# Self attention of a post-norm decoder layer: query and key projections issued in halves of the contraction, all projections spread over sixteen blocks

## What is computed

```python
# x, ctx: (8, 512, 256) float32; 16 heads of 16 channels
x = layernorm(x + self_attention(x, w_qkv, w_proj, b_proj, rel_bias_table))
x = layernorm(x + cross_attention(Q=x, K=ctx, V=ctx))      # no projections
x = layernorm(x + expert_ffn(x, centroids, ...))           # 8 experts, one for each token

def self_attention(x):
    qkv = x @ w_qkv.T                                       # (8, 512, 768)
    q, k, v = split into 16 heads of 16
    scores = q @ k.T * 0.25 + bias(rel_bias_table, distance)
    return softmax(scores) @ v @ w_proj.T + b_proj
```

## Time and profile before

| what | value |
|---|---|
| median of 3 runs | 1048.36 us (1044.22 to 1048.89) |
| span of the profiled execution, first to last instruction | 1045.2 us |
| PE busy | 934.1 us (89% of the span) |
| ACT busy | 747.5 us (72%) |
| DVE busy | 703.3 us (67%) |
| mean granted clock of TensorE | 0.951 of 2.4 GHz |
| self attention, by the first exponential of its batches | 37.3 to 418.5 us |
| cross attention | 418.5 to 715.5 us |

### The profile page before, as it was taken

The page is one execution under the profiler, slowest core; times in us unless marked ns, Lnnn a source line. Parts: engine busy times, 40 slices in busy tenths (PEclk is TensorE's granted clock), DMA queues, the critical chain, the costliest instruction groups (busy, mean ns, idle before and its releaser), DMA issues. The chain is left out here.

```text
span 1045.2 us, 17700 instructions
## 1 busy us (share of the span) xinstructions
PE 934.1 (89%) x5301; PEld 514.6 (49%) x5301; DVE 703.3 (67%) x1836; ACT 747.5 (72%) x1414; POOL 297.5 (28%) x337
## 2 busy tenths in 40 slices
PE   5599999999999999999999998996189999999991
PEld 2133444444444433333333333332179988988991
DVE  5277777677787788356556565585457887887883
ACT  1378777787878778899898895893047766766761
POOL 4043132231404111011222123123323534444443
PEclk9699999999999999999999997997589999999996
DMA  7989596978687675987876793751263533443450
GB/s 208 207 229 251 109 256 143 316 142 252 143 247 187 185 201 88 181 199 161 160 155 114 157 174 68 144 120 41 76 216 115 202 137 121 169 180 127 163 208 30
DMA packets 74844, 172.04 MB, mean 165 GB/s; under 512 B 16657, under 2 KB 36039, under 8 KB 64712
## 3 DMA queue, kind: packets, MB, share of 16 engines
q1 hardware_dynamic: 67944, 156.36, 60.4%
q0 software_dynamic: 6496, 14.16, 3.9%
q10 hardware_dynamic: 320, 0.52, 0.1%
HBM read 122.23 MB, written 53.73 MB: 168 GB/s over the span
## 5 line engine op out<-in xcount | busy, mean ns | idle before, releaser
L742 ACT ACTIVATE probs<-sc 128x512 f32<-128x512 f32 x1024 | 528.9, 608 | 117.7 <-DVE sc L829 80.4
L497 PE MATMUL sc<-qst,kst 57*128 57x512 f32 (+1 forms) x1024 | 268.4, 473 | 18.2 <-DMA qst<-s_qk 12.8
L829 DVE TENSOR_TENSOR sc<-sc,strip 128x308 f32<-128x308 f32 (+1 forms) x512 | 192.8, 430 | 101.2 <-PE sc L497 100.5
L509 PE MATMUL ot<-probs,vals 128*32 128x512 f32 x1600 | 214.0, 607 | 0.1
L497 PEld LDWEIGHTS sc<-qst,kst 57*128 57x128 f32 (+1 forms) x1024 | 118.6, 187 | 191.8 <-ACT probs L742 147.7
L1691 ACT ACTIVATE f_h<-f_h_ps,par 128x384 f32<-128x384 f32 x104 | 60.9, 586 | 31.0 <-PE f_h_ps L1601 31.0
L1768 DVE TENSOR_TENSOR f_h_lo<-f_h,f_h_hi 128x384 fp32r<-128x384 f32 x104 | 73.4, 706 | 13.7 <-DVE f_h_hi L1766 5.7
L1849 POOL DMA_INDIRECT home<-s_x,get_ids x45 | 53.6, 1190 | 72.5 <-issue 42.4
L1766 DVE CAST f_h_hi<-f_h 128x384 fp32r<-128x384 f32 x104 | 37.1, 356 | 39.7 <-ACT f_h L1691 39.5
L509 PE MATMUL ms<-probs,vals 128*32 128x512 f32 x448 | 61.9, 627 | 0.0
L1862 POOL DMA_INDIRECT out<-f_normed,f_put_ids x39 | 43.1, 1106 | 64.6 <-ACT f_normed L1725 56.1
(11 more groups left out here) (189 smaller groups left out, 1604.7 us busy)
## 6 DMA issues: line engine op xcount, KB each, us to landing
s_qk<-w_hi SPq DMA_DIRECT2D x32, 512.0 KB, 7.3
strip<-in_w_all SPq DMA_DIRECT2D x16, 1024.0 KB, 7.7
f_raw<-in_w_all SPq DMA_DIRECT2D x14, 1024.0 KB, 6.3
s_x<-x SPq DMA_DIRECT2D x8, 1026.0 KB, 11.0
kst<-s_qk SPq DMA_DIRECT2D x32, 256.0 KB, 6.1
qst<-s_qk SPq DMA_DIRECT2D x32, 256.0 KB, 7.2
s_x_parts<-split SPq DMA_DIRECT2D x16, 512.0 KB, 8.8
kst<-s_ctx_parts SPq DMA_DIRECT2D x32, 256.0 KB, 6.6
```

Source lines behind the costliest of these rows:

```text
L497: nc.tensor.matmul(sc[j][:], kst[at:at + rows, i, P * c:P * c + P], qst[at:at + rows, i, :], start=True, stop=True).then_inc(scored, 1)
L509: last = nc.tensor.matmul(sums_bank(n, g)[32 * j:32 * j + 32, :], vals[:, c, 4 * g + j, :], probs[:, k % KEPT, j, :], start=(c == 0), stop ...
L742: nc.scalar.activation(probs[:, k % KEPT, j, :], sc[j][:], ACT.Exp, scale=scale).then_inc(exped, 1)
L829: nc.vector.tensor_tensor(sc[j][:, lo:hi], sc[j][:, lo:hi], band_backwards(rank_of(4 * g + j), at, hi - lo), ALU.add).then_inc(biased, 1)
```

## The change

Seven things move, and nothing of the arithmetic is left out:
- A q or k tile is made in two parts, one half of the contraction at a time, in two different blocks. Tiles i = 0 and 1 of the next batch take blocks 0 to 3, tiles 2 and 3 blocks 12 to 15.
- ACT and DVE split these tiles in blocks 2, 4 and 15, and the last one in block 0 of the next batch. The store of tiles 2 and 3 and the load of pair 1 move behind it, into the batch that uses them.
- The v projections take blocks 8 to 11 and the output projection blocks 4 to 7, one block earlier each, and the DVE work behind them moves with them.
- The second group of transposes, `turn_x1(b, 0)`, moves from block 15 to block 1 of the next batch, with its copies in block 2.
- The x of batches 2 to 7 is loaded into the memory of `x2` (`later_xT`), and is split by halves behind `copy_v` on GpSimd.
- The last v tile and the transposes go through `ms2`.
- The waits on `ms` banks follow.

```diff
@@ -156,6 +156,7 @@
         x_hi, x_lo = sb("x_hi", [P, DC, N], F32R), sb("x_lo", [P, DC, N], F32R)
         w_qkv_lo = sb("w_qkv_lo", [P, DC, 3 * C], F32R)
         x2 = sb("x2", [P, NC, ROW])
+        later_xT = x2[:].rearrange("p t n -> p (t n)")[:, 0:DC * N].rearrange("p (d n) -> p d n", d=DC)
         centroids = sb("centroids", [P, DC, E])
         earlier = sb("earlier", [P, P], BF16)
         ones = sb("ones", [P, P], BF16)
@@ -382,30 +387,32 @@
                 if b > 0:
                     sp.wait_ge(xb_ready, b)
                     sp.dma_start(xnat[:], io["x"][b].rearrange("(c p) n -> p c n", p=P)).then_inc(ld_xnat, 16)
+                if b > 1:
+                    store_x1_parts(b - 2, 1)
+                if b > 0:
+                    store_parts(b, 2)
+                    store_parts(b, 3)
+                if b > 1:
+                    store_x1_parts(b - 2, 0)
+                if b > 0:
+                    load_pair(b, 1)
                 if b < B - 1:
                     store_parts(b + 1, 0)
                     store_parts(b + 1, 1)
                 else:
                     load_context(0)
                 store_ctx(b)
-                if b < B - 1:
-                    store_parts(b + 1, 2)
-                    store_parts(b + 1, 3)
                 load_pair(b + 1, 0)
                 if b < B - 1:
                     sp.wait_ge(st_ctx, 32 * (b + 1))
                     sp.dma_start(ctxT[:], io["ctxT"][b + 1].rearrange("(c p) n -> p c n", p=P)).then_inc(ld_ctx, 16)
+                if b < B - 2:
+                    wait(sp, x_lo_ready, DC * b)
+                    sp.dma_start(later_xT, io["xT"][b + 2].rearrange("(c p) n -> p c n", p=P)).then_inc(ld_xT, 16)
                 if b > 0:
                     store_x1(b - 1)
-                if b < B - 2:
-                    if b == 0:
-                        sp.wait_ge(v_mm, 4)
-                    else:
-                        sp.wait_ge(x_lo_ready, b)
-                    sp.dma_start(xT[:], io["xT"][b + 2].rearrange("(c p) n -> p c n", p=P)).then_inc(ld_xT, 16)
-                load_pair(b + 1, 1)
-                if b > 0:
-                    store_x1_parts(b - 1)
+                if b == B - 1:
+                    load_pair(B, 1)
                 if b == 1:
                     load_later()
                 if b == 2:
@@ -523,35 +534,44 @@
                     return [(w_qkv, xT, d) for d in range(DC)]
                 return [(w, x, d) for d in range(DC) for w, x in ((w_qkv_hi, x_hi), (w_qkv_hi, x_lo), (w_qkv_lo, x_hi))]
 
-            def project_qk(b, i):
-
-                if i == 0:
-                    wait(pe, ld_xT, 16 * b)
-                    wait(pe, x_lo_ready, b - 1)
-                    if b == 2:
-                        pe.wait_ge(w_halved, 1)
-                    wait(pe, v_nat, 2 * b)
-                elif i == 1:
-                    wait(pe, xt_lo, 2 * (b - 2))
-                else:
-                    wait(pe, qk_lo, 4 * b + i - 1)
+            def project_qk(b, i, d):
+
+                if d == 0:
+                    if i == 0:
+                        wait(pe, ld_xT, 16 * min(b, 1))
+                        if b == 2:
+                            pe.wait_ge(w_halved, 1)
+                        wait(pe, qk_lo, 4 * b - 1)
+                    elif i == 1:
+                        wait(pe, qk_lo, 4 * b)
+                    elif i == 2:
+                        pe.wait_ge(qk_lo, 4 * b + 1)
+                        wait(pe, out_read, 2 * (b - 1))
+                    else:
+                        pe.wait_ge(qk_lo, 4 * b + 2)
+                        wait(pe, v_nat, 2 * b + 1 if b > 0 else 0)
+                if i == 0 and b > 1:
+                    pe.wait_ge(x_lo_ready, DC * (b - 2) + d + 1)
                 col = C * (i % 2) + P * (i // 2)
-                terms = terms_of(b)
-                for n, (w, x, d) in enumerate(terms):
+                terms = [term for term in terms_of(b) if term[2] == d]
+                for n, (w, x, _) in enumerate(terms):
                     last = nc.tensor.matmul(ms[i % 2][:], w[:, d, col:col + P], x[:, d, :],
-                                            start=(n == 0), stop=(n == len(terms) - 1))
-                last.then_inc(qk_mm, 1)
+                                            start=(d == 0 and n == 0), stop=(d == DC - 1 and n == len(terms) - 1))
+                if d == DC - 1:
+                    last.then_inc(qk_mm, 1)
+                elif b > 0 and i == 3:
+                    last.then_inc(first_half_used, 1)
 
             def project_v(b, i, t):
 
-                if t == 0:
-                    wait(pe, qk_lo, 4 * b + 4 - i)
+                if t == 0 and i == 0:
+                    pe.wait_ge(qk_lo, 4 * b + (4 if b == 0 else 2))
                 if t == 0 and i == 1:
-                    wait(pe, out_read, 2 * (b - 1))
+                    wait(pe, out_read, 2 * b - 3)
                 tok = P * (2 * i + t)
                 terms = terms_of(b)
                 for n, (w, x, d) in enumerate(terms):
-                    last = nc.tensor.matmul(ms[1 - i][:, C * t:C * t + C], x[:, d, tok:tok + P], w[:, d, 2 * C:3 * C],
+                    last = nc.tensor.matmul(ms[1 + i][:, C * t:C * t + C], x[:, d, tok:tok + P], w[:, d, 2 * C:3 * C],
                                             start=(n == 0), stop=(n == len(terms) - 1))
                 if t == 1:
                     last.then_inc(v_mm, 1)
@@ -635,17 +659,23 @@
 
             def end_self(b, k):
 
-                if 5 <= k < 9:
-                    project_out(b, k - 5)
-                if k in (14, 15):
-                    turn_x1(b, 15 - k)
+                if k == 1 and b > 0:
+                    turn_x1(b - 1, 0)
+                if 4 <= k < 8:
+                    project_out(b, k - 4)
+                if k == 14:
+                    turn_x1(b, 1)
+                if k == 15 and b == B - 1:
+                    turn_x1(b, 0)
 
             def prepare_self(b, k):
 
                 if k < 4:
-                    project_qk(b, k)
-                if 9 <= k < 13:
-                    project_v(b, (k - 9) // 2, (k - 9) % 2)
+                    project_qk(b, k // 2, k % 2)
+                if 8 <= k < 12:
+                    project_v(b, (k - 8) // 2, k % 2)
+                if k >= 12:
+                    project_qk(b, 2 + k % 2, k // 14)
 
             def end_cross(c, k):
 
@@ -773,20 +804,24 @@
                 if exact:
                     peek(b)
                 for k in range(BLOCKS):
-                    if b < B - 1 and 1 <= k < 5:
-                        high_qk(b + 1, k - 1)
-                    if b < B - 1 and k in (11, 13):
+                    if b > 0 and k == 0:
+                        high_qk(b, 3)
+                    if b > 1 and k == 2:
+                        high_x1(b - 2, 0)
+                    if b < B - 1 and k in (2, 4, 15):
+                        high_qk(b + 1, (2, 4, 15).index(k))
+                    if b < B - 1 and k in (10, 12):
                         keep_v(b + 1, k // 2 - 5)
                     if b > 0 and k == 15:
                         high_x1(b - 1, 1)
                     exps(b, k)
-                    if b > 0 and k == 15:
-                        high_x1(b - 1, 0)
 
             def cross_body(c):
                 if exact:
                     peek(B + c)
                 for k in range(BLOCKS):
+                    if c == 0 and k == 2:
+                        high_x1(B - 2, 0)
                     if c == 0 and k == 15:
                         high_x1(B - 1, 1)
                     exps(B + c, k)
@@ -1102,7 +1137,9 @@
                     turn_sums(b, G - 1)
                 if k == 2:
                     divide_sums(b, G - 1)
-                if k == 7:
+                    if b > 0:
+                        low_x1(b - 1, 0)
+                if k == 6:
                     add_x(b, 0)
                 if k == 10:
                     merge_stats(b, 0)
@@ -1153,8 +1191,10 @@
                         turn_sums(b, k // 4 - 1)
                     if k in (6, 10, 14):
                         divide_sums(b, k // 4 - 1)
-                    if b < B - 1 and 1 <= k < 5:
-                        low_qk(b + 1, k - 1)
+                    if b > 0 and k == 0:
+                        low_qk(b, 3)
+                    if b < B - 1 and k in (3, 4, 15):
+                        low_qk(b + 1, (3, 4, 15).index(k))
                     if b > 0:
                         end_self_late(b - 1, k)
 
@@ -1334,12 +1374,15 @@
                 pool.wait_ge(w_hi_done, 1)
                 nc.gpsimd.tensor_tensor(w_qkv_lo[:], w_qkv[:], w_qkv_hi.bitcast(F32), ALU.subtract).then_inc(w_halved, 1)
 
-            def split_x(b):
+            def split_x(b, d):
                 pool.wait_ge(ld_xT, 16 * b)
-                wait(pool, v_mm, 2 * b)
-                nc.gpsimd.tensor_copy(x_hi[:], xT[:]).then_inc(x_hi_ready, 1)
-                pool.wait_ge(x_hi_ready, b - 1)
```

(34 more changed lines are left out.)

28 lines of the change are left out of this document (16 added, 12 removed).

## The result

The changed kernel took **1031.03 us** (median of 4 runs, 1028.82 to 1031.72), beside 1047.82 (4 runs, 1044.22 to 1048.89) for the kernel before: ratio 0.984, 95% interval 0.9801 to 0.9878. The forecast of 1035.5 lies 4.5 us above it, and the range holds it. The profiled execution took 1030.96 us, with a span of 1029.1: 16.1 us less than the span of before.

A forecast was written before the change was run, and what follows sets the result against it. Three engines (PE, ACT, DVE) waiting for each other in a ring bound the kernel. -12.3 (batches 1 to 6) - 1.5 (batch 0) + 1.0 (batch 7 and first cross batch) = -12.8, 1048.4 to 1035.5 us; range 1024 to 1046.

The forecast's parts named there:

- The batch anew: Batches 1 to 6: evenly loaded blocks take 46.4 us a batch instead of 48.45, -12.3 us in all.
- the ring's own 2.63: PE, ACT and DVE wait for each other; PE is held up in blocks with under 2.63 us of content.
- Stall (b) goes: A batch's first projection no longer waits for x_lo, 0.74 us (1.56 in batch 3); counted within the 48.45.
- x by halves: GpSimd's half splits of x, each under 2.4 us, are hidden behind PE's blocks.
- Rival 4: The x_lo wait stays because GpSimd's copies run late: 0.74 to 1.5 us in six batches, 1042 us; chance 0.05.
- The load of pair 1: Lands at +21 us of its batch, needed at block 8, +22; costed at nothing, 1 to 2 us of cover.
- rival 3: The load of pair 1 lands late, at +25: six batches lose 3 us each, 1053.5 us; chance 0.12.
- Batch 7 and the first cross batch: They take over the last q and k tile's split, four transposes and their copies: +1.0 us.
- Batch 0: Part of its half-clock first tile and some of three later tiles move to short late blocks: -1.5 us.
- Nothing else in the second and third stage moves: Beyond batch 7 and the first cross batch, the later stages keep their times: 0 us.
- Rivals 1, 2 and 5: Batches 1 to 6: ring keeps PE's gain, 1045 us (0.15); PE hardly waits, about 1018 (0.10); clock swings, 1052 (0.03).
- rival 5: Many short stalls in the first stage bring half-clock stretches on PE, costing 17 us, 1052 us; chance 0.03.

The follow-up runs named there:

- Experiment 2: Changed kernel with both halves of a q or k tile in one block (1, 3, 13, 15): 1039.27 us, ratio 0.9872.
- experiment 1: Kernel before plus only the early load of later x, split whole: ahead of GpSimd's copies 1065.15 us (ratio 1.0121), behind them 1047.04 us (0.9991).
- experiment 8: Kernel before with one more semaphore that nothing waits for: 1047.56 us; kernel before unchanged, profiled once more: 1053.79 us; one run each.
- experiment 3: Changed kernel with the load of later x back behind the store of x1 on SP: 1031.89 us, ratio 0.9813.
- Experiment 5: Changed kernel with GpSimd's split of the context put ahead of its copy of the last quarter of v: 1024.5 us, ratio 0.98.
- experiment 7: Changed kernel with GpSimd's copy of kept rows in the experts' stage put behind its inverse deviation: 1030.68 us, ratio 0.987.

## Why the prediction was right, step by step

- **The batch anew: right, shown.** 46.4 us was forecast and 46.4 measured in four batches, and each of the three sums of blocks came within 0.1 us. It came out even so by sums, not block by block: "nearly every one at the ring's own 2.63" is too simple, since the ten alike run from 2.56 to 3.06, depending on what DVE and ACT carry beside them. The six batches gave 11.8 of 12.3 us. Experiment 2 gives 6.5 of these to the halves.
- **"Stall (b) goes": the wait went, most of its gain did not.** I took 0.74 us for the wait of a quiet batch; it was batch 6's, and those of batches 2, 4 and 5 were 0.38 to 0.45 us and slack of the ring (experiment 1). Batch 6 gained some 0.4 us. Only in batches 1 and 3, where x came later still, did the path of x give more: 3.1 and 2.5 us with whole tiles (experiment 2). A part of batch 3's was the clock: with its wait of 1.56 us and 3.4 us at half clock it took 50.1, and with 1.34 and no half clock 48.3 (experiment 8). I had it within a mean of 48.45 us and priced no part of it alone, so that the sum survived.
- **x by halves: right, with more cover than I gave it** (experiment 3). Rival 4 is out.
- **The load of pair 1: cost at nothing, cost 1.1 us** in one batch of six. First issue at +9.0 (forecast +8.4), need at +22.0 (+22), last landing at +21.4 in batch 3 and +23.5 in batch 4 (+21). The cover was 0.6 us and not 1 to 2. This is rival 3, in one batch here and in none, one or two batches of the other kernels with that order on SP.
- **Batch 7 and the first cross batch: +1.0 was forecast, +2.8 measured, and the two can't be told apart.** The shown trace of the kernel before is the shortest of its order there; the middle ones of the old and the new order are 80.7 and 82.0 us, 1.3 apart. Steady is only the first cross batch, 36.7 to 36.8 before and 37.2 to 37.3 after. GpSimd's subtraction, which I did not count, was met before the change as well. Experiment 5 shows that this meeting costs batch 7 some 3 to 4 us in the new order; it doesn't show that the change brought it.
- **Batch 0:** -1.2 for -1.5, but both lie within what batch 0 varies by.
- **"Nothing else in the second and third stage moves": wrong by 5 us**, in the forecast's favour. No instruction was moved and the copy still starts 0.45 us after `f_h_lo`, but `f_h_lo` is stretched in 7 tiles instead of 13. What tips it is open: not the number of semaphores, and not the place of x in memory, since both kernels of experiment 1 kept the long stage. Without it the measured difference of spans would be 11.0 us, and without the part ahead of batch 0 too 8.7, against 12.8 forecast. The stages that the forecast's sum is made of gave 10.2 us of the 12.8. So the batch's length was foreseen; that the whole gain came out larger than forecast, and not 2.6 us smaller, is luck: 5.1 us of the experts' stage and 2.3 ahead of batch 0, less 1.6 in the seven cross batches.
- **Rivals 1, 2 and 5** did not come: batches neither at 48 nor at 43.5, and a granted clock of 1.00 from 81 to 360 us (0.99 before). The rule of the Trainium skill that was weighed with rival 5 ("TensorE: Matmul & The Clock Gate", section A second HAM failure mode: psum-queue depth-cycling) isn't borne out by the trace here either: with more and smaller groups the clock did not move. The half-clock stretch behind the longest pause of the second stage is there in both kernels, its batch 45.1 us long in the changed one.

## What to carry to other kernels

Where three engines wait for each other in a ring, work that one of them carries beside the ring belongs in equal pieces into every turn: a wait of 0.4 us was worth nothing here, and evening out the short and long turns 1.2 us a batch. Price a transfer moved behind other issues with the slowest issue, not the median one. And of each DVE instruction ask what GpSimd runs at that time, whether the change moves it or not: two lines swapped on GpSimd, the engine with the most room, gave 5.7 us against the trace shown (1.9 in six batches, 3.8 in one), most of it at a meeting that was there before the change. Where a stage's difference is a few microseconds, look at a second trace of the kernel before: its batch 7 took 42.8 us in one and 46.3 in the other.

## What the runs showed of the hardware

- A DVE instruction whose operands all lie in SBUF and that met a GpSimd instruction ended, in these cases, some 0.2 to 0.4 us after GpSimd's: `normed` 0.42 to 1.54 us beside a subtraction of 2.36; a pair of norms 0.73 to 2.79; `f_h_lo` 0.56 to 1.72 beside a plain copy of 0.84; a cast (`f_h_hi`) 0.36 to 0.99. DVE's bands, which take one operand from PSUM, weren't stretched: 0.84 us for two at 365.89, in the middle of the subtraction. Nor were the sums for the norm (`f_stats_out`, one input, 0.41 us each) beside the copy in the tiles that weren't stretched.
- It goes the other way too: GpSimd's copy, 0.84 us by itself, took 1.59 to 1.76 us in eleven tiles of experiment 7 and 1.08 in one, each time beside a DVE subtraction of 1.22 us that had started 0.15 to 0.8 us earlier. The cast behind that subtraction then took 0.99 us instead of 0.36.
- By the records the one that starts first does not always win: `f_h_lo` had started 0.45 us before the copy and was stretched, in eleven tiles of one kernel, and in another kernel with the same distance in five only.
- One issue of a load on SP took 1.83 us where its kind takes 0.58, and the same load then landed 8.9 us after its issue instead of 8.0.
